# Rests of GpSimd between indirect transfers in the relation layers: every third transfer, and none in the last group

## The reference

```
x = x + L0(h)   # four rounds: y = segment_sum(weight * y[src], dst)
x = x + L1(h)   # message = sum over 16 basis products * (h[src] @ W[k]), summed over dst
x = x + L2(h)   # two relational convolutions and a log_softmax
x = x + L3(h)   # tensor-product message, summed over dst, then an update of the node
```

```
out[i] = h[i] @ root + bias + sum over edges e into i of  norm[e] * (h[src[e]] @ W[type[e]])
norm[e] = 1 / max(number of edges into i of type[e], 1)
```

## Time and profile before

| what | value |
|---|---|
| timed runs, median of 3 | 18782.5 us (18770.41 to 18819.21) |
| profiled execution | 18798.8 us |
| its span | 18797.0 us |
| granted TensorE clock, mean over the span | 0.881 |
| TensorE busy | 15061.3 us (80%) |
| VectorE busy | 14607.7 us (78%) |
| ScalarE busy | 11866.0 us (63%) |
| GpSimd busy | 10732.2 us (57%) |

### The profile page before, as it was taken

One profiled execution on the slowest core, in us unless ns is written; L12 is line 12 of the kernel. 1 busy time (PEld: TensorE's weight loads), 2 busy tenths in 40 slices (PEclk: granted clock), 3 DMA queues, 4 the chain that ended last, 5 costly groups with the idle time before them and its releaser, 6 DMA issues. The chain is left out here.

```text
span 18797.0 us, 353555 instructions
## 1 busy us (share of the span) xinstructions
PE 15061.3 (80%) x83251; PEld 13368.1 (71%) x83252; DVE 14607.7 (78%) x36172; ACT 11866.0 (63%) x23181; POOL 10732.2 (57%) x33516
## 2 busy tenths in 40 slices
PE   0158828887887888788699988999919999689997
PEld 0058828887887888788688885777607777489996
DVE  4845557777777777777699997999808888689997
ACT  2000027776776777677577777888718888567775
POOL 0468837775775775777477706666652243477720
PEclk9555559998998999899899998999959999899998
DMA  7611120000000000000111112222201122111111
GB/s 226 122 28 39 39 75 23 22 22 22 22 22 22 22 22 23 21 22 23 31 31 31 31 24 64 70 70 72 66 18 60 64 66 65 42 31 30 30 27 17
DMA packets 1258063, 826.18 MB, mean 44 GB/s; under 512 B 863939, under 2 KB 1202983, under 8 KB 1250343
## 3 DMA queue, kind: packets, MB, share of 16 engines
q1 hardware_dynamic: 865126, 670.89, 12.9%
q0 software_dynamic: 274432, 117.81, 3.5%
q10 hardware_dynamic: 118080, 33.61, 1.0%
HBM read 586.84 MB, written 234.66 MB: 44 GB/s over the span
## 5 line engine op out<-in xcount | busy, mean ns | idle before, releaser
L1534 PE MATMUL powers_sums<-powers_b_hot,powers_spread 128*128 128x224 f32 x26400 | 5269.3, 364 | 1047.1 <-DVE powers_b_hot L1515 1000.9
L1534 PEld LDWEIGHTS powers_sums<-powers_b_hot,powers_spread 128*128 128x128 f32 x26400 | 5160.7, 197 | 1158.0 <-issue 1114.1
L1619 POOL DMA_INDIRECT filled<-powers_by_b,powers_at_start x2912 | 3548.1, 1218 | 1918.7 <-issue 865.3
L2299 PE MATMUL relate_got<-relate_hot,relate_table 112*128 112x512 f32 (+1 forms) x10560 | 3076.9, 434 | 68.9 <-ACT relate_hot L2261 68.9
L1529 ACT ACTIVATE powers_b_hot<-powers_away,ones 128x672 f32<-128x672 f32 x2640 | 1981.8, 753 | 1600.3 <-PE powers_sums L1534 1393.6
L1523 ACT ACTIVATE powers_away<-wide,powers_minus_b 128x224 f32<-128x224 f32 x6600 | 2719.2, 472 | 117.4 <-ACT powers_minus_b L1687 37.6
L2299 PEld LDWEIGHTS relate_got<-relate_hot,relate_table 112*128 112x128 f32 x10560 | 1697.6, 191 | 1340.9 <-issue 1269.1
L1512 DVE TENSOR_TENSOR powers_spread<-powers_a_hot,powers_message 128x640 f32<-128x640 f32 x2640 | 2157.8, 817 | 233.7 <-PE powers_sums L1534 138.8
L2261 ACT ACTIVATE relate_hot<-relate_away,ones 112x1280 f32<-112x1280 bf16 x1320 | 1799.4, 1363 | 508.1 <-PE relate_got L2299 453.7
L1515 DVE TENSOR_SCALAR powers_b_hot<-wide,powers_b_val 128x224 f32<-128x224 f32 x6600 | 1940.5, 343 | 0.0
L2314 PE MATMUL relate_mixed<-relate_mix,relate_picked 128*128 128x128 f32 x13200 | 1704.2, 276 | 39.4 <-DVE relate_picked L2363 39.4
(11 more groups left out here) (473 smaller groups left out, 26115.0 us busy)
## 6 DMA issues: line engine op xcount, KB each, us to landing
relate_codes<-pair_rows SPq DMA_DIRECT2D x264, 800.0 KB
powers_given<-filled SPq DMA_DIRECT2D x528, 200.0 KB
rec<-relate_running SPq DMA_DIRECT2D x132, 400.0 KB
filled<-powers_by_b,powers_at_start POOLq DMA_INDIRECT x2912
grouped<-order_blanks POOLq DMA_DIRECT2D x20, 1320.0 KB
filled<-order_blanks SPq DMA_DIRECT2D x20, 1320.0 KB
held_recs<-grouped SPq DMA_DIRECT2D x132, 200.0 KB
conv_given<-filled SPq DMA_DIRECT2D x132, 200.0 KB
```

Source lines behind the costliest of these rows:

```text
L1534: mm = pe.matmul(gathering.sums[:, bass.ds(group * STRIDE, WINDOW)], spread[:, j].rearrange("p a d -> p (a d)"), b_hot[:, j, :], start=Fal ...
L1619: pool.indirect_dma_start(filled, bass.IndirectOffsetOnAxis(at_start[0:n, k, a, i:i + 1], 0), g.by_b[0:n, k, a * D:(a + 1) * D], None).the ...
L2299: mm = pe.matmul(got[:, n % 2, at:to], table[:, n // SLOTS % 2, half, :], flat[:, at:to], start=half == 0, stop=half == 1, skip_group_chec ...
```

## The change

The relation layers get a constant of their own, `TYPE_BURST` = 3: GpSimd rests ahead of every third transfer in the type transfers and in the ends. In the ends of the last of the seven groups it doesn't rest at all. `rest` takes the number of its memsets from the width of the scratch tile, which is still 10 in every layer.

```
+TYPE_BURST = 3
...
-    for k in range(RESTS):
+    for k in range(still.shape[1]):
         ins = pool.memset(still[:, k:k + 1], 0.0)
...
                     for a in range(8):
-                        if (block * 8 + a) % CALM_BURST == 0 and block + a:
-                            rest(pool, still, rested, rests_upto(block, a, CALM_BURST), gate)
+                        if (block * 8 + a) % TYPE_BURST == 0 and block + a:
+                            rest(pool, still, rested, rests_upto(block, a, TYPE_BURST), gate)
                         pool.indirect_dma_start(inverses.filled, bass.IndirectOffsetOnAxis(at_start[0:n, k, a, i:i + 1], 0),
                                                 type_rows[0:n, k, a * T:(a + 1) * T], None).then_inc(spread_out[block % 2], 16)
...
-            rests = rests_upto(SPREAD_BLOCKS, -1, CALM_BURST) if count_types else 0
+            rests = rests_upto(SPREAD_BLOCKS, -1, TYPE_BURST) if count_types else 0
...
                 for h in range(HI):
-                    if h % CALM_BURST == 0:
-                        rest(pool, still, rested, rests + g * -(-HI // CALM_BURST) + h // CALM_BURST + 1, gate)
+                    if h % TYPE_BURST == 0 and g < GROUPS - 1:
+                        rest(pool, still, rested, rests + g * -(-HI // TYPE_BURST) + h // TYPE_BURST + 1, gate)
                     pool.indirect_dma_start(to[:, h, :], None, sums, bass.IndirectOffsetOnAxis(G.ends[:, h, g:g + 1], 0)
                                             ).then_inc(ends_in, 16)
```

## The result

The changed kernel takes 18599.62 us (median of 4 runs, 18597.99 to 18603.49), the kernel before 18799.08 us beside it (18770.41 to 18819.21). The ratio is 0.9895, 95% interval 0.9878 to 0.9912: faster by 199 us, or 1.1%. The forecast was 18495 us, in 18460 to 18560, and a gain of 287 us. The direction is right, the size is 88 us short, and the time lies above the range.

What follows compares the result with a forecast made beforehand. GpSimd was taken to set the first relation layer's end and, by its last group, the second's. Savings of 107.2 + 127.6 + 43.1 us in rests and 9.6 in pauses, 287.5 off 18782.5, gave 18495 us, range 18460 to 18560.

Steps and rivals of the forecast that it cites:

- The bound: First relation layer: GpSimd's strand sets the end, VectorE idling 405.79 us; second: only the last group's 174 us count.
- The price of a rest and their count: Relation layers: 315 rests fewer on the path, at 0.886 us in type transfers and 0.88 in ends, 277.9 us.
- The pauses: GpSimd's occasional longer idling between ends: goes with instructions issued; 3.5 pauses of 2.75 us vanish, 9.6 us.
- Transfers at 1.25 us without a rest: Unrested runs on GpSimd: transfers keep the pace of six gathers seen in a row; nothing more taken.
- The rival of a queue that does not keep up: Unrested runs: each transfer past the second costs extra; at 1.30 us each, 526 us slower, 19309 us; 3%.
- What is late next: First layer: GpSimd still ends 161 us after the loop; last group starts 106 us after its stored sums.
- a sign of being wrong: First relation layer: a longer matmul loop there would show the forecast wrong; no size given.
- Denser transfers beside other work: Matmul loops beside busier GpSimd: no cost to TensorE or VectorE taken; upper bound 16 us over a loop.
- Rival 3: First layer: contention slows the loop, last group's stored sums come late, group starts 94 us later; 18589 us; 4%.
- The upper bound by way of VectorE's two-input instructions: Loop: were denser transfers to block VectorE's two-input instructions, 106 us must be used up before it showed.

Runs made afterwards that it cites:

- after_again: The changed kernel run once more, unaltered, in place 5: 18518.2 us, ratio 0.9860 to the kernel before.
- e2: The kernel before, resting at every second transfer, but with no rest in the last group of both relation layers: 18767.8 us, ratio 0.9991.

## Why the prediction was wrong

- *The bound.* Right. GpSimd set the end of the first layer in every run: the layer outlasted its loop by 68 to 358 us in all the variants.
- *The price of a rest and their count.* Right: 315 rests on the path at 0.88 us (6380 rest memsets in the two layers, as forecast), and with the pauses 286.8 us saved in the two layers in after_again, against 287.5 in the sum; but the two profiles are from two places. Where nothing was held up the times of 18501 to 18518 us lie in the forecast's range.
- *The pauses.* Right: in the first layer GpSimd idles for over 2.5 us without a releaser 13 times before (44.0 us) and 10 times after (34.3 us), so 9.7 us have gone, where 9.6 were taken for both layers. That they go with the count of instructions is not shown.
- *Transfers at 1.25 us without a rest.* Right: the steps are 1.25 us in the changed kernel's run of 98, and a group of 98 takes 125 to 126 us in place 4 and in place 6. The rival of a queue that does not keep up falls, also where the loop was held up.
- *What is late next.* Right for the first layer: GpSimd still sets its end, though the loop there grew by 50 us, which the prediction had named as a sign of being wrong. For the second it missed the loop itself.
- *Denser transfers beside other work.* This is the step that failed. It took nothing, with 16 us as its upper bound, from stretches of before in which GpSimd rested with every second transfer. Those rows hold for runs of two; I carried them over to runs of three to five, and to a run of 98 beside the loop's last 68 us. In the place of the timing it cost the loop 118 us, of which 107 had been GpSimd's tail anyway; instead of -44 the second layer came out at +13, 57 us short, and the loss moved the layer's end from GpSimd to the matmul loop. In the first layer the loop lost 50 us under its cover, and GpSimd's gain was 19 us less than forecast there, 14 of them in longer transfers. The other 15 us are in layers that the change doesn't touch: `powers` ended anywhere from 9090 to 9136 us in the profiles of the runs above.
- *Rival 3* was the nearest: a loop slowed by contention. I put it in the first layer, where there was cover, and priced it at 94 us; it struck in the second, where GpSimd's tail behind the loop was 107 us and the run of 98 lay beside the loop's end. The upper bound by way of VectorE's two-input instructions, which the Trainium skill's rule (SBUF — State Buffer, section Who interferes with whom) suggested, was beside the point: it is about VectorE, and in this trace TensorE and ScalarE stopped together with it.

The question that I did not ask is what the rests were there for. The earlier trace rows show a busy TensorE beside a resting GpSimd, and say nothing of a GpSimd that doesn't rest.

## What to carry to other kernels

A pause that looks like waste may keep another engine going. Before it is taken out beside a busy loop, ask what it protects, and take it out first where nothing runs at its side, as in the first layer's last group: that layer became 49 us shorter in e2, in a place where the loop was held up. Measure a change of this kind in more than one place: the same kernel gained 1.1% in one and 1.4 to 1.5% in three others, each with a spread of under 0.2% within the place. Where the engines stop and nothing in the program explains it, see whether the traces of fast and slow places hold the same number of records. And a bound taken from rows holds only for the pattern in those rows.

## What the runs showed of the hardware

- Indirect transfers of GpSimd, issued one behind the other at 1.25 us with nothing between, can stop TensorE, VectorE and ScalarE together: 118 to 123 us of a run of 130 us in places 1 and 2. Where that happens, three ends in a row cost nothing, and five in a row 64 of 150 us (place 4). Beside type transfers in threes, with some runs of four and five, TensorE stopped for up to 5.2 us at a time, and the first layer's loop lost 37 to 50 us in places 1 and 2 and 117 in place 4.
- In three of seven places (5, 6 and 7) it did not happen at all, with no rest in 98 transfers, and in a fourth (3) not in runs of up to twelve.
- The traces of the places where it happened lack some four in ten of the semaphore records that the others have, from the early layers on. Whether recording is the cause is not shown.
- In a hold-up the start of a VectorE instruction lay 24.5 us behind the end of the matmuls that it waits for, and matmuls without a wait came one per 2.8 us. Late signals alone would not explain the second, if the profile has all that these matmuls wait for. The path that they share with GpSimd's issue was not found.
